# A vision tower with routed experts: 24 products of the identity with itself placed on TensorE between the first expert's list and its first gathered rows

## What is computed

```
h = tok(x)                                    # (64, 37, 256)
h = h + attn(layernorm(h))
# ffn on layernorm(h), rows flattened to N = 2368, capacity = 444
probs = softmax(x @ router_w + router_b); topv, topi = top_k(probs, 2)
pv, pp = top_k(where(expert chosen, gate, -1), capacity)     # per expert
xin = x_flat[pp // 2]                         # gather
h1 = gelu(xin @ w1 + b1)                      # 256 -> 1024, per expert
out_e = (h1 @ w2 + b2) * w                    # 1024 -> 256
out = zeros.at[tok].add(out_e);  out = layernorm(out) * ln_g + ln_b
```

## Time and profile before

| | us |
|---|---|
| median of 3 runs | 432.01 (429.76 to 432.26) |
| the profiled execution, its time | 430.07 |
| the profiled execution, first to last instruction (span) | 428.3 |
| mean granted TensorE clock over the span | 0.901 |

### The profile page before, as it was taken

How to read it: one execution, slowest core, us unless ns; L and a number is a source line. 1 busy time by engine, 2 the same in 40 slices (tenths; PEclk the granted TensorE clock), 3 DMA queues, 4 the chain that set the end, 5 groups by cost and what they waited for, 6 DMA issues and landing times.

```text
span 428.3 us, 8091 instructions
## 1 busy us (share of the span) xinstructions
PE 350.5 (82%) x2190; PEld 312.2 (73%) x2190; DVE 318.4 (74%) x864; ACT 259.3 (61%) x548; POOL 245.8 (57%) x438
## 2 busy tenths in 40 slices
PE   2789999999999999440035999999999999999910
PEld 0587999899999987330024899999999999999700
DVE  7667878788778757689987456787888888888660
ACT  3365777777877856355500577777777777777400
POOL 4157888878788864501304333458686768655561
PEclk9899999999999999755555799999999999999975
DMA  6631125454454596669504566559595959552220
GB/s 182 181 73 63 43 66 145 135 142 134 126 137 126 119 98 158 160 155 206 1 0 116 154 185 186 161 144 254 160 257 162 261 160 257 163 168 69 60 64 21
DMA packets 49278, 58.38 MB, mean 136 GB/s; under 512 B 12167, under 2 KB 38007, under 8 KB 49244
## 3 DMA queue, kind: packets, MB, share of 16 engines
q1 hardware_dynamic: 42602, 43.11, 39.1%
q0 software_dynamic: 5568, 14.09, 12.3%
q10 hardware_dynamic: 1074, 0.79, 0.7%
HBM read 36.74 MB, written 21.36 MB: 136 GB/s over the span
## 4 chain that ended last, share of the span: by engine, by line
PE 74%; DVE 11%; issue 4%; POOL 3%; SPq 3%; DMA 2%; ACT 2%; POOLq 0%; DVEq 0%; ACTq 0%
PE pz L944 18%; PE pall L961 17%; PE pall L829 10%; PE pall L779 5%; PE pall L786 4%; PE pz L759 3%; DVE wproj L1228 2%; PE pall L804 2%; PE pall L812 2%; SPq L442 2%; PE pall L795 2%; PE pall L839 2%; PE pall L972 1%; PE pall L831 1%; PE pall L930 1%
## 5 line engine op out<-in xcount | busy, mean ns | idle before, releaser
L961 PE MATMUL pall<-halves 128*128 128x448 f32 x384 | 89.8, 369 | 0.8 <-DVE halves L1334 0.8
L944 PE MATMUL pz<-halves 128*128 128x448 f32 x384 | 90.3, 372 | 0.0
L944 PEld LDWEIGHTS pz<-halves 128*128 128x128 f32 x384 | 73.7, 192 | 6.0
L961 PEld LDWEIGHTS pall<-halves 128*128 128x128 f32 x384 | 71.1, 189 | 6.9 <-DVE halves L1334 1.1
L712 ACT ACTIVATE wproj<-pz,b1t 128x448 f32<-128x448 f32 x64 | 40.7, 636 | 47.0 <-PE pz L944 42.1
L1334 DVE TENSOR_TENSOR halves<-wproj,halves 128x448 fp32r<-128x448 f32 x64 | 40.2, 629 | 31.6 <-ACT halves L724 22.7
L829 PE MATMUL pall<-halves 128*112 128x256 f32 x396 | 53.0, 289 | 3.3 <-DVE halves L1055 3.3
L1582 POOL DMA_INDIRECT held<-x_rows,gidx x32 | 33.8, 1056 | 38.2 <-DVE gidx L1276 13.7
L1481 POOL TENSOR_TENSOR rs<-rs,neghalf 112x1 f32<-112x1 f32 x88 | 50.2, 570 | 7.3
L1607 POOL DMA_INDIRECT out<-rows,didx x28 | 37.1, 1325 | 25.2 <-DVE rows L1382 15.5
L829 PEld LDWEIGHTS pall<-halves 128*112 128x112 f32 x396 | 48.7, 179 | 3.7 <-DVE zbias L1074 2.4
(11 more groups left out here) (267 smaller groups left out, 745.8 us busy)
## 6 DMA issues: line engine op xcount, KB each, us to landing
stage<-in_w SPq DMA_DIRECT2D x32, 512.0 KB
stage<-in_x SPq DMA_DIRECT2D x64, 108.0 KB
x_rows<-x SPq DMA_DIRECT2D x22, 224.0 KB, 2.9
x_rows<-held SPq DMA_DIRECT2D x22, 224.0 KB, 4.3
sums<-rows SPq DMA_DIRECT2D x7, 448.0 KB
out<-held SPq DMA_DIRECT2D x21, 111.0 KB
x_rows<-zero SPq DMA_DIRECT2D x1, 1474.9 KB
wproj<-in_w_proj ACTq DMA_DIRECT2D x1, 768.0 KB
```

The costliest lines, as they stand in the source:

```text
L944: m = nc.tensor.matmul(bank(k % 2)[:, 0:SLOTS], w[:, c, k * 128:(k + 1) * 128], xs[:, e % 2, c, :], start=(n == 0), stop=(n == 3 * EC - 1))
L961: m = nc.tensor.matmul(pall[:, 2 * (e % 2) + o, 0:SLOTS], w[:, k, o * 128:(o + 1) * 128], hs[:, k % 2, :], start=(k == 0 and n == 0), stop ...
```

## The change

A function `keep_clock(n)` is added on TensorE. It issues n products of the identity with itself, fp32, 128 by 128 by 128 columns, each started and stopped by itself, into the first 128 columns of bank 3. It waits for nothing and signals nothing, and no one reads its result. It is called once, with 24, after the products of L904 and ahead of `first_gathered(0)`.

```diff
@@ -905,6 +905,11 @@
                                      start=(q == 0), stop=(q == TILES - 1))
             m.then_inc(r_list, 1)
 
+            def keep_clock(n):
+
+                for _ in range(n):
+                    nc.tensor.matmul(bank(3)[:, 0:128], ident[:, :], ident[:, :], start=True, stop=True)
+
             def lists(h):
                 pe.wait_ge(r_val, h + 3)
                 for q in range(h * Q // 2, (h + 1) * Q // 2):
@@ -974,6 +979,7 @@
                     if j % 2 or e == E - 1:
                         m.then_inc(y_ps, 1)
 
+            keep_clock(24)
             for h in range(2):
                 first_gathered(h)
                 lists(h)
```

## The result

The kernel with the burst takes 428.91 us (median of 16 runs, 427.90 to 430.64) against 431.16 us (16 runs) for the kernel before in the same comparison. The ratio is 0.9948, with a 95% interval of 0.9931 to 0.9965: 2.2 us or half a percent faster, and clear of the noise. A second comparison of the unchanged pair, with 6 runs against 17, gave 0.9953 (0.9935 to 0.9971). The profiled execution took 428.84 us with a span of 427.1.

A forecast was written before the change was run, and what follows sets the result against it. TensorE was taken as the bound from 235.86 on, the experts' first 12 products running at half clock. Gains of 0.65 + 1.2 + 0.25 = 2.1 us took 432.01 to 429.9, own range 428.3 to 431.3, 8 in 10 427.9 to 432.7.

The forecast's parts named there:

- The sum: Up to the first expert's second group of products: three gains of 0.65, 1.2 and 0.25 make 2.1 us.
- the earlier start of `hidden`: The experts' first 12 products, L944, start at about 235.2 instead of 235.86: 0.65 us gained, between 0.2 and 0.8.
- the fast `hidden(0, 0)`: At full clock the first Gelu starts 1.42 us after L944's first product instead of 2.62: 1.2 us gained.
- the first projection's group: The first group of L961 takes 1.22 us at full clock instead of 1.47: 0.25 us gained.
- The chain Gelu to projection: Gelu, rounding and remainder on ScalarE and VectorE take 2.14 us, independent of TensorE's clock.
- the pause of 1.1 us foreseen: TensorE finishes `hidden(0, 1)` at 237.6 and waits 1.1 us for the first projection at 238.8.
- The burst: Behind L904: 48 instructions from 224.13, 20 slow at 0.21 us and 28 fast at 0.11, ending at 231.5.
- Does the clock stay?: Weak step: full clock lasts through 3.7 us of transposes and list products before L944, and a later 1.1 us pause.
- Rises and falls: Rival: clock falls again before or around 235; gain 0.3 to 1.3, about 0.8 us, giving 431.2; chance 0.25.
- the second rival: Wording in the 8-in-10 range sentence for a case that, with no change, lies within 427.9 to 432.7.
- Never rises: Rival: the added products do not raise the clock; L944 starts 3.9 us later, giving 435.9; chance 0.07.
- Gained and lost again: Rival: a weight load, gather or an expert's scatters set a later point; 432.0; chance 0.13 together with something else.

The follow-up runs named there:

- burst ahead alone: Kernel with the 24 products plus 12 more ahead of L904's wait, VectorE's order unchanged; against the kernel before: 431.65 us, ratio 1.0017.
- transposes: Kernel before plus 48 one-instruction transposes of the identity in place of the change's 24 products; 430.07 us, ratio 0.9969 against the kernel before.
- 36: Kernel before plus 36 identity products behind L904 instead of the change's 24; 431.05 us, ratio 1.0003 against the kernel before.
- fillers: The change plus 4, 7, 2 and 7 products in TensorE's pauses at the end of the tiles; 428.26 us, ratio 0.9942 against the kernel before.
- VectorE's order alone: The change plus expert 0's list copy moved ahead of the reduction L1278 on VectorE; 429.07 us, ratio 0.9958 against the kernel before.
- all together: The change plus products at the end of the tiles, 12 ahead of L904 and VectorE's list copy moved earlier; 427.97 us, ratio 0.9931 against the kernel before.
- both edits: The change plus 12 products ahead of L904's wait and VectorE's list copy moved ahead of its reduction; 428.77 us, ratio 0.9947 against the kernel before.
- 18: Kernel before plus 18 identity products behind L904 instead of the change's 24; 428.82 us, ratio 0.9972 against the kernel before.
- both edits again: Second comparison of the kernel with 24 products, 12 ahead of L904 and VectorE's list copy moved earlier; 428.35 us, ratio 0.9931 against the kernel before.
- 12: Kernel before plus 12 identity products behind L904 instead of the change's 24; 430.28 us, ratio 0.9989 against the kernel before.

## Why the prediction was right, and where it was not

**The sum.** It said 2.1 us; the profiles' stage gives 1.98, the two comparisons 2.2 and 2.0. By its terms: the earlier start of `hidden` 0.65 said, 0.72 measured; the fast `hidden(0, 0)` 1.2 said, 1.10 measured (237.08 - 235.56 = 1.52 to the Gelu against 2.62); the first projection's group 0.25 said, 0.16 measured (240.53 - 239.22 = 1.31). The chain Gelu to projection is 2.14 us in both profiles, and the pause of 1.1 us foreseen is 0.95. So the mechanism is the one that was forecast, term by term. The second profile of the change, in which the burst ended later and no wait for rows was left, gives a smaller sum: its first projection starts 14.95 us behind L904's end, 1.54 earlier than before instead of 1.82.

**The absolute time.** 429.9 was said, 428.91 came. The median I worked from, of three runs, was 0.85 above that of the sixteen; the rest is 0.1. The absolute number was thus off by the choice of its starting point, and not by the sum.

**The profile's own difference** is only 1.2 us (428.3 to 427.1), although the stage gives 1.98. The routing came 0.42 later in this execution (224.55 against 224.13), 0.06 lies behind the last group of L966, and 0.30 in the experts: some 14 groups of six products there took 1.24 instead of 1.22 us. What slowed those groups is open. They are also in some of the experiments, and not in others.

**The burst.** Its start at L904's end and its 48 instructions: right. The rise was put 3.0 to 5.5 us after its start, 4.3 taken. It was 3.5 in this profile, so that some 16 instructions and not 20 ran slow, and 2.8 to 6.1 over all eleven profiles with fp32 products. The bounds came from two rises, and the measured spread is wider. The slow pace of 0.21 was right, though I had taken it from L751, where the granted clock reads 1.00 and only the pace says half. The fast pace of 0.11 came as said: where all 48 are fast, as in the version with the burst ahead alone, their row is 5.60 us long. List products at full clock, which no row had shown, are (233.01 - 231.88) / 22 = 0.051 each: a little over half of 0.092, not the 0.06 I took.

**Does the clock stay?** It did in both profiles of the change. The one row for it was a pause of 0.77 us among dense products, and others stood against it, so that the step held was in part luck. The experiments tie it to where the burst ends, within limits that they leave wide. Burst's end (start plus length of its row) to the first product of `hidden`, over all twelve bursts:

| gap, us | profiles | clock when `hidden` starts |
|---|---|---|
| 3.2 to 3.9 | 6 (the change twice, transposes, 36, fillers, VectorE's order alone) | full in all |
| 4.9, 5.0 | 2 (all together; both edits) | full in both |
| 5.2 to 8.2 | 4 (18, both edits again, burst ahead, 12) | half in all |

The clean parting of the rows is in part made by the clock itself, as a fall ahead of `hidden` slows the lists and so lengthens the gap. In the two profiles with both edits the transposes of the second half start 2.84 us behind the burst's end alike; that the gap is 5.0 in one and 5.7 in the other came of the fall at 231.6. With 18 the last lists took 1.61 us instead of 1.30, and without that its gap too would be 4.9. So at about 5 us of such work both outcomes occur, and the table gives no limit. Nor is a short gap shown to be safe: in the second profile with both edits the clock fell 3.1 us after the burst, and the change's own gap was 3.2 in one profile and 3.9 in the other. With 12 and 18 products and with the burst ahead it fell 4.5 to 5.6 us after. So a loss in some executions of the change is not ruled out; its two profiles show none.

**The rivals.** "Rises and falls" is real, though in the change itself it was not seen; where it was seen, the first projection came 0.1 us (12) and 0.7 (18) earlier than before, against the 0.3 to 1.3 of gain that I gave it. The sentence on the range calls it "the second rival"; it is the first in the list, and the 435.9 of the second lies outside 427.9 to 432.7. "Never rises" fell with the change's own profile, and the evidence that I gave for it was one execution read as a rule, as the transposes show. "Gained and lost again" is not seen, save the 0.30 us above.

## What to carry to other kernels

Where a trace shows the first products of a dense stretch of TensorE at half clock behind a pause, filler products in the pause can buy that back. The gain is bounded by what runs slow on the path, here 1.1 us of Gelu's start and 0.9 us around it. In this kernel the filler had to end close ahead of the dense work and not behind the data it waits for: 12 products were too few, 36 too many. One that gets the full clock earlier ends earlier, so its number has to be set again after each change ahead of it. And one profile of a version is one execution: two of the same kernel differed in the very thing that the filler is for. Work out from the timeline what the next engine in the chain makes of it: of the 2.1 us that the twelve products themselves became shorter, 1.1 reached the Gelu.

## What the runs showed of the hardware that I had not expected

Transposes bring the full clock too: 48 of the identity, at 1.2 GHz from 225.9, ran at 2.4 GHz from 231.9, and the kernel's own 22 transposes did it in two of the profiles. The delay between the start of steady work and the rise varied from 2.8 to 6.1 us between executions. The fall varied as much: 5.4, 4.5, 5.6 and 3.1 us after the burst's end in the four profiles in which it came before `hidden`, with the sparse transposes and list products of this stage in between. One kernel kept the clock in one execution and lost it in another.
